# A transformer block on eight cores: where the recurrent scan is cut between the part that runs alone and the part that runs inside the expert layer

## The chip, the cores and the metric

The kernel runs on all 8 cores of one Trainium2 chip. Each core takes one element of the batch (2048 tokens of width 1024) and works alone; nothing is exchanged. The metric is the device time of the slowest core in microseconds (us). The kernel before takes 8822.76 us, the median of three runs (8819.5 to 8960.93).

## The reference, cut to what matters

```
x = layernorm(x + scan_layer(x))          # L0: linear recurrence with tanh, state 128
x = layernorm(x + moe(x))                 # 8 experts, 1024 -> 4096 -> 1024, top 2 of 8
x = layernorm(x + attention(x))           # 16 heads, causal
x = layernorm(x + ffn(x))                 # r * (relu(k)^2 Wv)

def step(state, inp):                     # scan_layer, 2048 steps one after the other
    u_t, sp_t = inp
    state = tanh(state @ A.T + u_t @ B.T) + sp_t
    return state, state @ C.T             # then out = ys @ Wo.T + bo

h = relu(einsum('nd,edh->neh', x_flat, w1) + b1)   # moe: all 8 experts for every token
y = einsum('neh,eho->neo', h, w2) + b2
out = einsum('ne,neo->no', dense_gate, y)
```

Token t of the scan needs token t-1. Everything behind the scan (the output product, the layernorm, the gate, the experts) works on tokens one by one, so tokens whose scan is done can go on while later ones are still being scanned.

## The kernel before, in words

Activations lie with the feature on the partitions: `xA` and `xB` are [128, 8, 2048] fp32, `xS` is the bf16 copy that matmuls read. Tokens are handled in four tiles of 512 (`TS`). Every instruction is written down by the helper `E`, which takes the engine, the operation, the semaphores that it waits for (`w`) and the one it raises (`s`). `realize` then plays one list per engine in the order in which they were written, so the order of the code is the order of every engine's queue. All instructions therefore carry one line number in the profile (L978); groups are told apart by tile names.

- P1: `u`, `sp` and the bias of each step `c` = B u + A sp (shifted by one token) are computed for all 2048 tokens. `sp` and `c` lie in two halves of 1024 columns each (`sp_a`, `sp_b`, `c_a`, `c_b`).
- P2: `scan_step(t)` is one matmul of AT with one column of `tanh_bf` into one of two PSUM columns (TensorE, waits for semaphore `act`), and one tanh of it with bias c into the next column of `tanh_bf` (ScalarE, waits for `spe`). Steps 0 to 1023 run by themselves.
- The loop `for ch in (0, 1)` then takes 1024 tokens (two tiles) at a time through `l0out` (state, C, Wo, residual), `emit_ln` (layernorm), `gate` (router) and `moe`.
- `moe(ch)` walks through 16 halves (8 experts, the hidden width in two halves of 2048). In each half it loads 4 MB of `w1b` and 4 MB of `w2b` (8 DMAs each, counted in bf16, from POOL's queue, each waiting for the one before), and for each tile of the chunk makes 128 matmuls with `w1b` (16 groups of 8, each group evicted through relu by ScalarE and VectorE in turn into `hbuf`) and 128 matmuls with `w2b` (8 groups of 16, evicted by VectorE into `xB`). I call the first 128 the w1 section and the other 128 the w2 section. `w1b` and `w2b` have one buffer each: the next `w1_load` waits for the last w1 matmul of the half (`mm1`), `w2_load` for the last w2 eviction of the half (`ye`). All weights are loaded once for each chunk.
- In chunk 0, `moe` calls `hook()` after each of the 24 groups of a tile. `hook` calls `scan_pump`, which writes as many scan steps as are due: 1024 steps over 768 calls. Steps 1024 to 2047 are so put between the groups of chunk 0's experts. Chunk 1 has no hooks.
- Before chunk 1, columns 1024 to 2047 of `xA` are loaded again by SyncE, and CT2 and WoB2 by POOL, since `moe` had used their place.
- After both chunks: layernorm, attention, feed-forward layer, layernorm, store.

Of the kernel before, what the change touches and what calls it, by code (L numbers as in the profile page):

```python
# [5 lines left out]
F32 = mybir.dt.float32  # L6
# [20 lines left out]
def build(stage=None):  # L27
# [79 lines left out]
    BT = place("BT_s", [128, 128], BF16, W_OFF + 14592)  # L107
    CT = place("CT_s", [128, 128], BF16, B_OFF + 28928)
    CT2 = place("CT2_s", [128, 128], BF16, A_OFF)
    WoB2 = place("WoB2", [128, D], BF16, A_OFF + 256)  # L110
    ident = place("ident_s", [128, 128], F32, W_OFF + 17408)
    zsq0 = place("zsq0", [128, T], BF16, W_OFF)
    zsq1 = place("zsq1", [128, T], BF16, W_OFF + 4096)
# [20 lines left out]
    sp_a = place("sp_a", [128, 1024], F32, B_OFF + 8192)
    sp_b = place("sp_b", [128, 1024], F32, B_OFF + 4096)
    c_a = place("c_a", [128, 1024], F32, B_OFF + 16384)
    c_b = place("c_b", [128, 1024], F32, B_OFF + 12288)
# [122 lines left out]
    for nt in range(NT):  # L260
        b = 2 + nt % 2
        lo = nt * TS
        for dk in range(NCH):
            E("tensor", "matmul", bank(b), WsB[:, dk, :], xS[:, dk, lo:lo + TS],
              start=(dk == 0), stop=(dk == NCH - 1),
              w=((("evs", max(0, V("evs") - 1)),) if dk == 0 else ()),
              s=("mms" if dk == NCH - 1 else None))
        E("vector", "tensor_scalar_add",
          sp_h[nt // 2][:, (nt % 2) * TS:(nt % 2) * TS + TS], bank(b), bsS,
          w=(("mms", V("mms")),), s="evs")  # L270
    E("vector", "tensor_copy", out=sp_bf[:, 0:1024], in_=sp_a,
      w=(("evs", V("evs")),))
    E("vector", "tensor_copy", out=sp_bf[:, 1024:2048], in_=sp_b, s="spb")
    for nt in range(NT):
        b = 4 + nt % 2
        lo = nt * TS
        E("tensor", "matmul", bank(b), BT, u_bf[:, lo:lo + TS], start=True, stop=False,
          w=(("evu", 4), ("spb", V("spb")), ("evc", max(0, V("evc") - 1))))
        if nt == 0:
            E("tensor", "matmul", bank(b)[:, 1:TS], AT, sp_bf[:, 0:TS - 1],  # L280
              start=False, stop=True, s="mmc")
        else:
            E("tensor", "matmul", bank(b), AT, sp_bf[:, lo - 1:lo + TS - 1],
              start=False, stop=True, s="mmc")
        E("vector", "tensor_copy",
          out=c_h[nt // 2][:, (nt % 2) * TS:(nt % 2) * TS + TS], in_=bank(b),
          w=(("mmc", V("mmc")),), s="evc")
    barrier()

# [1 line left out]

    def scan_step(t):
        if t == 0:
            E("scalar", "activation", tanh_bf[:, 0:1], c_a[:, 0:1], AF.Tanh,
              s="act", chain=False)
            return
        cbias = c_h[t // 1024][:, t % 1024:t % 1024 + 1]
        E("tensor", "matmul", ssb[t % 2], AT, tanh_bf[:, t - 1:t],
          start=True, stop=True, w=(("act", t),), s="spe")
        E("scalar", "activation", tanh_bf[:, t:t + 1], ssb[t % 2],  # L300
          AF.Tanh, bias=cbias, w=(("spe", t),), s="act", chain=False)

    mark("P2_scan")
    for t in range(0, 1024):
        scan_step(t)
    scan_cursor = [1024]

    def scan_pump(nsteps):
        t0 = scan_cursor[0]
# [3 lines left out]
        scan_cursor[0] = t1  # L313

    def l0out(ch):
        lo2 = ch * 1024
        E("vector", "tensor_add", state_bf[:, lo2:lo2 + 1024],
          tanh_bf[:, lo2:lo2 + 1024], sp_h[ch],
          w=(("act", 1024 * (ch + 1)),), s="stb")
        stb_t = V("stb")  # L320
        CTu = CT if ch == 0 else CT2
        WoBu = WoB if ch == 0 else WoB2
        for sub in range(2):
            nt = 2 * ch + sub
            b = sub
            lo = nt * TS
            E("tensor", "matmul", bank(b), CTu, state_bf[:, lo:lo + TS],
              start=True, stop=True,
              w=(("stb", stb_t), ("evy", max(0, V("evy") - 1)),
                 ("ldc2", V("ldc2"))), s="mmy")  # L330
            E("scalar", "activation", ys_bf[:, lo:lo + TS], bank(b), AF.Copy,
              w=(("mmy", V("mmy")),), s="evy")
        evy_t = V("evy")
        for o in range(NCH):
            for sub in range(2):
                nt = 2 * ch + sub
                b = 2 + (o * 2 + sub) % 2
                lo = nt * TS
                E("tensor", "matmul", bank(b), WoBu[:, o * 128:(o + 1) * 128],
                  ys_bf[:, lo:lo + TS], start=True, stop=True,  # L340
                  w=(("evy", evy_t), ("evz", max(0, V("evz") - 1))), s="mmz")
                E("vector", "scalar_tensor_tensor", xB[:, o, lo:lo + TS], bank(b),
                  boS[:, o:o + 1], xA[:, o, lo:lo + TS], ALU.add, ALU.add,
                  w=(("mmz", V("mmz")), ("ldx2", V("ldx2"))), s="evz")
        E("vector", "drain", s="l0d")
# [54 lines left out]
        E("vector", "drain", s="lnd")  # L400

    def gate(ch):
        tt0 = 8 * ch
        for tt in range(tt0, tt0 + 8):
            b = 4 + tt % 2
            pt = bank(b)[:, 0:NE]
            lo = tt * 128
            for dk in range(NCH):
                E("tensor", "matmul", pt, xA[:, dk, lo:lo + 128], gwS[:, dk, :],
                  start=(dk == 0), stop=False,  # L410
                  w=((("ggl", max(0, V("ggl") - 1)), ("apl", V("apl")))
                     if dk == 0 else ()))
# [3 lines left out]
        gp3 = gscr[:, 0:64].rearrange("p (t e) -> p t e", t=8)
        gm3 = gscr[:, 512:576].rearrange("p (t e) -> p t e", t=8)
        gx = gscr[:, 256:264].rearrange("p (t o) -> p t o", o=1)
        gv = gscr[:, 768:776].rearrange("p (t o) -> p t o", o=1)
        gsl = glall[:, tt0:tt0 + 8, :]  # L420

        def bc8(ap):
            return ap.to_broadcast([128, 8, NE])

        E("vector", "reduce_max", gx, gsl, AX.X, s="gmx")
        E("vector", "tensor_tensor", gp3, gsl, bc8(gx), ALU.subtract)
# [7 lines left out]
        E("vector", "reduce_max", gv, gm3, AX.X)  # L434
        E("vector", "tensor_tensor", gm3, gp3, bc8(gv), ALU.is_ge)
        E("vector", "tensor_mul", gsl, gp3, gm3, s="gtile")
        for tt in range(tt0, tt0 + 8):
# [6 lines left out]
        E("vector", "tensor_copy", out=xB[:, :, ch * 1024:(ch + 1) * 1024],  # L444
          in_=xA[:, :, ch * 1024:(ch + 1) * 1024], s="zin")

    def w1_load(e, half, w=()):
        for dk in range(NCH):
# [15 lines left out]
    HALVES = [(e, h) for e in range(NE) for h in range(2)]  # L464

    def moe(ch, hook=None):
        nts = (2 * ch, 2 * ch + 1)
        w1_load(HALVES[0][0], HALVES[0][1], w=(("zin", V("zin")),))
        for hi, (e, half) in enumerate(HALVES):
            w1_tgt = V("w1l")  # L470
            ye_at_start = V("ye")
            w2_load(e, half, w=(("ye", ye_at_start),))
            if half == 0:
                cl = ch * 1024
                E("sync", "dma_start", out=row0[:, cl:cl + 1024],
                  in_=g8[e:e + 1, cl:cl + 1024],
                  w=(("gbc", V("gbc")),), s="grw", n=16)
# [591 lines left out]
```

How the kernel before makes its waits and increments, by code:

```python
    def run(eng_obj, lst):  # L969
        eng_key = [k for k, v in ops.items() if v is lst][0]
        for method, args, kw, w, s, n in lst:
            for sn, v in w:
                if v > 0:
                    eng_obj.wait_ge(sems[sn], v)
            if method == "wait_":
                names[eng_key].append(None)
                continue
            ins = getattr(eng_obj, method)(*args, **kw)
            names[eng_key].append(ins.ins.name)
            if s is not None:
                ins.then_inc(sems[s], n)
```

## Time and profile before

| what | us |
|---|---|
| median of 3 runs | 8822.76 |
| lowest, highest | 8819.5, 8960.93 |
| the profiled execution | 8840.08 |
| its span, slowest core (5) | 8838.5 |
| other cores' spans | 8809.8 to 8837.8 |

Busy time of core 5: TensorE matmuls 5711.6 us (65% of the span), weight loads 2411.4, VectorE 2787.7, ScalarE 1527.7, POOL 406.5. The span is read by stage. A row of the windows view gives start and end of the stretch, its length, then the busy time (and number of instructions) of TensorE's matmuls, its weight loads, VectorE, ScalarE and POOL, then the mean granted TensorE clock (1.00 is 2.4 GHz, 0.50 is 1.2 GHz), the mean busy share of the 16 DMA engines, and GB/s. A timeline row gives the start, the duration, the instruction with its count, and in brackets how long the engine had been idle and what released it.

### The profile page before, as it was taken

The numbers are of one execution on the slowest core, as the hardware profiler recorded it, in microseconds if no ns is written. First come the engines' busy times: TensorE is split into PE (matmuls) and PEld (weight loads), VectorE is DVE, ScalarE is ACT, GpSimd is POOL, SyncE is SP. The second block draws the span as 40 slices with busy tenths as digits, with TensorE's granted clock in tenths as the row PEclk, the third lists the DMA queues.
The fourth block names the chain that finished last, engine by engine and source line by source line (L and its number), as shares of the span: only waits on it lengthen the run. The fifth ranks groups of instructions, "written<-read, shape, count | busy, mean of one in ns | idle before, by whom it ended". The sixth has DMA issues, their size and how long they took to land.

```text
span 8838.5 us, 83477 instructions; the slowest of 8 cores (8809.8 to 8838.5 us)
## 1 busy us (share of the span) xinstructions
PE 5711.6 (65%) x24427; PEld 2411.4 (27%) x24427; DVE 2787.7 (32%) x4295; ACT 1527.7 (17%) x3342; POOL 406.5 (5%) x612
## 2 busy tenths in 40 slices
PE   2223588787878785788787878844556455645455
PEld 1112233333333332333333333311112111211122
DVE  0002222222222223222222222245454555455544
ACT  2332111111111111000000000012222211221111
POOL 0000000000000000000000000000000000000000
PEclk6555899999999996899898989965656555655667
DMA  1000333424243430434334343300000000000012
GB/s 44 0 0 0 56 59 51 65 46 65 45 65 48 63 53 26 72 53 62 62 53 71 54 67 57 59 8 8 10 10 5 6 10 10 5 5 5 0 19 48
DMA packets 237365, 319.62 MB, mean 36 GB/s; under 512 B 66198, under 2 KB 197782, under 8 KB 234902
## 3 DMA queue, kind: packets, MB, share of 16 engines
q0 software_dynamic: 226560, 284.33, 21.6%
q1 hardware_dynamic: 10390, 29.94, 1.1%
q8 instruction: 238, 3.90, 0.2%
q14 instruction: 177, 1.45, 0.1%
HBM read 581.62 MB, written 8.39 MB: 67 GB/s over the span
## 4 chain that ended last, share of the span: by engine, by line
PE 42%; DMA 25%; DVE 15%; issue 10%; ACT 7%; DVEq 1%; ACTq 0%; POOLq 0%; SPq 0%; PEldq 0%
PE psA L978 35%; DMA w1b<-w 15%; DMA w2b<-w 8%; PE psB L978 7%; DVE mcols L978 4%; ACT tanh_bf L978 4%; ACT PT L978 2%; DVE xA L978 2%; DVE Qpair L978 1%; DVE qraw L978 1%; DVE mtmp L978 1%; DVE rowT L978 1%; DVE mcol L978 1%; ACT rowT L978 1%; DVE xB L978 1%
## 5 line engine op out<-in xcount | busy, mean ns | idle before, releaser
L978 PE MATMUL psA<-xS,w1b 128*128 128x512 bf16 x8192 | 1880.4, 388 | 566.4 <-DMA w1b<-w 551.7
L978 PE MATMUL psA<-hbuf,w2b 128*128 128x512 bf16 x8192 | 1820.5, 382 | 150.7 <-DVE hbuf L978 73.4
L978 PEld LDWEIGHTS psA<-xS,w1b 128*128 128x128 bf16 x8192 | 775.7, 99 | 1522.7 <-issue 670.2
L978 DVE TENSOR_SCALAR hbuf<-psA,b1c 128x512 bf16<-128x512 f32 x512 | 384.4, 751 | 2260.3 <-PE psA L978 2260.3
L978 PEld LDWEIGHTS psA<-hbuf,w2b 128*128 128x128 bf16 x8192 | 784.8, 98 | 1119.8 <-issue 219.9
L978 PE MATMUL psB<-tanh_bf,AT_s 128*128 128x1 bf16 x2047 | 337.7, 165 | 725.7 <-ACT tanh_bf L978 725.7
L978 ACT ACTIVATE hbuf<-psA,b1c 128x512 bf16<-128x512 f32 x512 | 351.8, 687 | 1631.9 <-PE psA L978 1630.4
L978 ACT ACTIVATE tanh_bf<-psB,c_b 128x1 bf16<-128x1 f32 x1024 | 268.0, 262 | 1307.9 <-PE psB L978 1307.9
L978 ACT ACTIVATE PT<-psA 128x512 bf16<-128x512 f32 (+3 forms) x448 | 308.4, 688 | 1023.0 <-PE psA L978 1011.4
L978 PEld LDWEIGHTS psB<-tanh_bf,AT_s 128*128 128x128 bf16 x2047 | 206.7, 101 | 944.8 <-issue 856.6
L978 DVE SCALAR_TENSOR_TENSOR ytmp<-psA,b2c,g_sb 128x512 f32<-128x512 f32 x256 | 192.3, 751 | 637.6 <-PE psA L978 637.6
L978 DVE SCALAR_TENSOR_TENSOR ytmp<-psA,g_sb 128x512 f32<-128x512 f32 x256 | 177.1, 692 | 648.9 <-PE psA L978 648.9
L978 DVE TENSOR_TENSOR xB<-xB,ytmp 128x512 f32<-128x512 f32 x512 | 354.6, 693 | 55.7 <-DVE ytmp L978 3.2
L978 PE MATMUL psA<-Qh,Kh 65*128 65x512 bf16 (+3 forms) x640 | 258.3, 475 | 164.0 <-ACT PT L978 116.8
L978 ACT ACTIVATE tanh_bf<-psB,c_a 128x1 bf16<-128x1 f32 x1023 | 269.6, 264 | 419.3 <-PE psB L978 419.3
L978 POOL DMA_DIRECT2D w1b<-w x256 | 136.1, 532 | 3878.2 <-PE psA L978 1663.8
L978 PE MATMUL psA<-Kh,Qh 64*128 64x512 bf16 (+1 forms) x320 | 129.0, 524 | 202.3 <-DVE mcols L978 118.5
L978 POOL DMA_DIRECT2D w2b<-w x256 | 190.1, 743 | 1360.6 <-DMA w2b<-w 1152.3
L978 PE MATMUL psB<-PT,Vg 128*65 128x512 bf16 (+3 forms) x640 | 231.4, 471 | 16.9 <-DVE PT L978 7.8
L978 ACT ACTIVATE g_sb<-psB 128x512 f32<-128x512 f32 x64 | 38.2, 597 | 1153.2 <-DVE xB L978 867.0
L978 PE MATMUL psA<-aout,wub 64*128 64x512 bf16 x512 | 219.7, 629 | 22.1 <-DVE aout L978 22.1
L978 PE MATMUL psB<-Kh,Qh 64*128 64x512 bf16 (+1 forms) x320 | 142.7, 567 | 131.6 <-DVE mcols L978 128.4
(157 smaller groups left out, 3685.6 us busy)
## 6 DMA issues: line engine op xcount, KB each, us to landing
w1b<-w POOLq DMA_DIRECT2D x256, 512.0 KB, 5.3
w2b<-w POOLq DMA_DIRECT2D x256, 512.0 KB, 5.4
xA<-xT SPq DMA_DIRECT2D x8, 1024.0 KB, 17.0
out<-ost SPq DMA_DIRECT2D x8, 1024.0 KB, 12.7
xA<-xT SPq DMA_DIRECT2D x8, 512.0 KB, 8.6
Qh<-Qpair SPq DMA_DIRECT2D x16, 256.0 KB, 3.5
Kh<-Qpair SPq DMA_DIRECT2D x16, 256.0 KB, 3.7
wqb<-WqT POOLq DMA_DIRECT2D x16, 128.0 KB, 3.2
```

What stands on the lines that cost most here:

```text
L978: ins = getattr(eng_obj, method)(*args, **kw)
```

## The change

The scan is cut at 512 steps, not at 1024, and the chunks are tiles (0) and (1, 2, 3), not (0, 1) and (2, 3). Steps 0 to 511 run by themselves; the other 1536 are put into chunk 0's experts, which now work on one tile. `hook()` is also called after each of the 8 matmuls of a w1 group, so that there are 16 x 152 = 2432 calls (in each tile of a half 16 x 9 in the w1 section and 8 in the w2 section). `l0out`, `gate` and `moe` take their tiles from `CH_NTS`. `sp` and `c` lie in four pieces of 512 columns, at places that chunk 0 does not write; WoB2 moves to a place that the reload of `xA` (now columns 512 to 2047) leaves free.

```
-    WoB2 = place("WoB2", [128, D], BF16, A_OFF + 256)
+    WoB2 = place("WoB2", [128, D], BF16, A_OFF + 8192)
...
+    CH_NTS = ((0,), (1, 2, 3))
     mark("P2_scan")
-    for t in range(0, 1024):
+    for t in range(0, TS):
         scan_step(t)
-    scan_cursor = [1024]
+    scan_cursor = [TS]
...
     def l0out(ch):
-        lo2 = ch * 1024
-        E("vector", "tensor_add", state_bf[:, lo2:lo2 + 1024],
-          tanh_bf[:, lo2:lo2 + 1024], sp_h[ch],
-          w=(("act", 1024 * (ch + 1)),), s="stb")
-        stb_t = V("stb")
+        nts = CH_NTS[ch]
...
+        for i, nt in enumerate(nts):
+            lo = nt * TS
+            E("vector", "tensor_add", state_bf[:, lo:lo + TS],
+              tanh_bf[:, lo:lo + TS], sp_n[nt],
+              w=((("act", (nts[-1] + 1) * TS),) if i == 0 else ()), s="stb")
...
     def moe(ch, hook=None):
-        nts = (2 * ch, 2 * ch + 1)
+        nts = CH_NTS[ch]
...
                           s=("mm1" if dk == NCH - 1 else None))
+                        if hook is not None:
+                            hook()
...
                 E("sync", "dma_start", out=xA[:, c, TS:T],
                   in_=xT[c * 128:(c + 1) * 128, TS:T], s="ldx2", n=16)
...
-            ngroups = 16 * 2 * 24
+            nhooks = 16 * len(CH_NTS[0]) * (16 * 9 + 8)
             per = [0]
 
             def hook(per=per, ch=ch):
                 if ch == 0:
                     per[0] += 1
-                    tgt = 1024 + (1024 * per[0]) // ngroups
+                    tgt = TS + ((T - TS) * per[0]) // nhooks
                     scan_pump(tgt - scan_cursor[0])
```

TensorE's queue in chunk 0's experts before, from the end of one half into the w1 section of the next (`tanh_bf,AT_s` is a scan step, `w1b` and `w2b` are the experts):

```order
L978 MATMUL psA<-hbuf,w2b 128x512 [waits w2b,ye,hes,hev]
L978 MATMUL psA<-hbuf,w2b 128x512 x15
L978 MATMUL psB<-tanh_bf,AT_s 128x1 [waits act] x2
L978 MATMUL psB<-brow_g,ones_rb 128x512 [waits gcv]
L978 MATMUL psA<-xS,w1b 128x512 [waits w1l,hes]
L978 MATMUL psA<-xS,w1b 128x512 x7
L978 MATMUL psB<-tanh_bf,AT_s 128x1 [waits act]
L978 MATMUL psA<-xS,w1b 128x512 [waits w1l,hev]
```

The same queue now, two groups of a w1 section:

```order
L987 MATMUL psA<-xS,w1b 128x512 [waits w1l,hev]
L987 MATMUL psB<-tanh_bf,AT_s 128x1 [waits act]
L987 MATMUL psA<-xS,w1b 128x512 x2
L987 MATMUL psB<-tanh_bf,AT_s 128x1 [waits act]
L987 MATMUL psA<-xS,w1b 128x512
L987 MATMUL psB<-tanh_bf,AT_s 128x1 [waits act]
L987 MATMUL psA<-xS,w1b 128x512 x2
L987 MATMUL psB<-tanh_bf,AT_s 128x1 [waits act]
L987 MATMUL psA<-xS,w1b 128x512 x2
L987 MATMUL psB<-tanh_bf,AT_s 128x1 [waits act] x2
L987 MATMUL psA<-xS,w1b 128x512 [waits w1l,hes]
```

Where one or two scan steps stood behind every eighth matmul, one now stands behind every first or second. In the w2 section a step still stands only behind a group of 16.

ScalarE's queue there before, and now (`hbuf` is a relu, waiting for its group by `mm1`):

```order
L978 ACTIVATE tanh_bf<-psB,c_b 128x1 [waits spe] x2
L978 ACTIVATE hbuf<-psA,b1c 128x512 [waits mm1,act]
L978 ACTIVATE tanh_bf<-psB,c_b 128x1 [waits spe] x3
L978 ACTIVATE hbuf<-psA,b1c 128x512 [waits mm1,mm2,act]
L978 ACTIVATE tanh_bf<-psB,c_b 128x1 [waits spe] x14
```

```order
L987 ACTIVATE tanh_bf<-psB,c_n_114 128x1 [waits spe] x5
L987 ACTIVATE hbuf<-psA,b1c 128x512 [waits mm1,act]
L987 ACTIVATE tanh_bf<-psB,c_n_114 128x1 [waits spe] x11
L987 ACTIVATE hbuf<-psA,b1c 128x512 [waits mm1,mm2,act]
L987 ACTIVATE tanh_bf<-psB,c_n_114 128x1 [waits spe] x12
```

Between two relus there are now 11 or 12 tanhs where there were 2 or 3; behind the last relu of a tile there are 12 (the rest of the w1 section and the w2 section) where there were 14.

## Rows read from the trace of the kernel before

**Rows 1.** Cores: the slowest, its span and mean granted clock.
```profile
core 5: 8838.5 us, clock 0.768
```

**Rows 2.** Windows by stage: lone scan; chunk 0 before and in experts; chunk 1 likewise.
```profile
83.40:772.00 688.60, 167.09 (x1023) 106.48 (x1023) 0.00 (x0) 269.42 (x1023) 0.00 (x0) 0.50 0.00 0
772.00:954.80 182.80, 72.00 (x227) 41.08 (x228) 59.92 (x100) 14.06 (x16) 4.27 (x8) 0.56 0.14 23
954.80:3366.50 2411.70, 1916.05 (x9246) 854.33 (x9246) 557.86 (x774) 437.42 (x1311) 158.83 (x248) 0.95 0.36 55
3366.50:3569.10 202.60, 73.07 (x229) 41.35 (x230) 61.03 (x102) 14.15 (x16) 5.31 (x10) 0.55 0.20 43
3569.10:5787.00 2217.90, 1848.20 (x8222) 811.90 (x8223) 557.57 (x773) 194.40 (x287) 158.84 (x248) 0.92 0.39 59
```

**Rows 3.** Timeline, TensorE, second tile of one half of chunk 1's experts.
```profile
3771.19 27.80 PE L978 MATMUL psA<-xS,w1b 128*128 128x512 bf16 x128
3800.13 27.79 PE L978 MATMUL psA<-hbuf,w2b 128*128 128x512 bf16 x128 [1.15 <-DVE hbuf L978]
3830.58 0.37 PE L978 MATMUL psB<-brow_g,ones_rb 1*128 1x512 bf16 x1 [2.66 <-DVE brow_g L978]
3845.58 29.07 PE L978 MATMUL psA<-xS,w1b 128*128 128x512 bf16 x128 [14.62 <-DMA w1b<-w]
```

**Rows 4.** Timeline, POOL, the same half: first w1b, first and last w2b issue behind it.
```profile
3799.60 0.54 POOL L978 DMA_DIRECT2D w1b<-w  x1 [49.44 <-PE psA L978]
...
3845.88 0.75 POOL L978 DMA_DIRECT2D w2b<-w  x1 [5.25 <-DMA w1b<-w]
...
3889.20 0.74 POOL L978 DMA_DIRECT2D w2b<-w  x1 [5.29 <-DMA w2b<-w]
```

**Rows 5.** Timeline, chunk 0's experts: a w1b load, and the matmul behind it.
```profile
1364.21 0.54 POOL L978 DMA_DIRECT2D w1b<-w  x1 [62.40 <-PE psA L978]
...
1411.77 3.22 PE L978 MATMUL psA<-xS,w1b 128*128 128x512 bf16 x8 [15.68 <-DMA w1b<-w]
```

**Rows 6.** Timeline, a step of the lone scan, TensorE.
```profile
85.40 0.16 PE L978 MATMUL psB<-tanh_bf,AT_s 128*128 128x1 bf16 x1 [0.51 <-ACT tanh_bf L978]
```

**Rows 7.** Timeline, relu, tanh and the scan step waiting for it, chunk 0's experts.
```profile
1418.70 0.69 ACT L978 ACTIVATE hbuf<-psA,b1c 128x512 bf16<-128x512 f32 x1 [1.56 <-PE psA L978]
1419.28 0.26 ACT L978 ACTIVATE tanh_bf<-psB,c_b 128x1 bf16<-128x1 f32 x1
...
1419.68 0.16 PE L978 MATMUL psB<-tanh_bf,AT_s 128*128 128x1 bf16 x1 [1.19 <-ACT tanh_bf L978]
...
1419.92 0.38 PE L978 MATMUL psA<-xS,w1b 128*128 128x512 bf16 x1
```

**Rows 8.** Timeline, TensorE, a waited-for step ahead of a w2 group; a step between groups.
```profile
1383.93 0.16 PE L978 MATMUL psB<-tanh_bf,AT_s 128*128 128x1 bf16 x1 [0.54 <-ACT tanh_bf L978]
1384.37 3.61 PE L978 MATMUL psA<-hbuf,w2b 128*128 128x512 bf16 x16 [0.28 <-issue]
1387.82 0.17 PE L978 MATMUL psB<-tanh_bf,AT_s 128*128 128x1 bf16 x1
1387.85 3.61 PE L978 MATMUL psA<-hbuf,w2b 128*128 128x512 bf16 x16
```

**Rows 9.** Timeline, chunk 0's first w1 group, at the low clock.
```profile
954.81 3.57 PE L978 MATMUL psA<-xS,w1b 128*128 128x512 bf16 x8 [43.75 <-DMA w1b<-w]
...
958.18 0.21 PE L978 MATMUL psB<-tanh_bf,AT_s 128*128 128x1 bf16 x1
```

**Rows 10.** Windows (columns as in rows 2): an experts tile, l0out, the feed-forward layer.
```profile
1415.00:1478.70 63.70, 55.94 (x276) 25.21 (x275) 15.70 (x22) 12.53 (x38) 5.19 (x7) 1.00 0.45 65
...
3389.00:3401.00 12.00, 7.93 (x15) 1.36 (x13) 10.28 (x14) 0.00 (x0) 0.00 (x0) 0.50 0.00 0
8449.00:8509.00 60.00, 60.00 (x229) 24.84 (x228) 0.00 (x0) 17.23 (x29) 6.11 (x7) 0.81 0.32 31
```

**Rows 11.** Timeline, the first matmul of chunk 1's l0out.
```profile
3386.20 1.01 PE L978 MATMUL psA<-state_bf,CT_s 128*128 128x512 bf16 x2 [19.51 <-DMA WoB<-WoT]
```

More of the change, by code:

```diff
@@ L133, in build @@
     u_bf = place("u_bf", [128, T], BF16, B_OFF)
[L134 to L137, printed above, removed]
+    sp_n = [place("sp_n0", [128, TS], F32, B_OFF + 8192),
+            place("sp_n1", [128, TS], F32, B_OFF + 4096),
+            place("sp_n2", [128, TS], F32, B_OFF + 6144),
+            place("sp_n3", [128, TS], F32, B_OFF + 45056)]
+    c_n = [place("c_n0", [128, TS], F32, B_OFF + 16384),
+           place("c_n1", [128, TS], F32, B_OFF + 12288),
+           place("c_n2", [128, TS], F32, B_OFF + 14336),
+           place("c_n3", [128, TS], F32, B_OFF + 36864)]
     tanh_bf = place("tanh_bf", [128, T], BF16, B_OFF + 20480)
     sp_bf = place("sp_bf", [128, T], BF16, B_OFF + 24576)
-    sp_h = (sp_a, sp_b)
-    c_h = (c_a, c_b)
     w1b = place("w1b", [128, NCH, 2048], BF16, A_OFF)
@@ L267, in build @@
               s=("mms" if dk == NCH - 1 else None))
-        E("vector", "tensor_scalar_add",
-          sp_h[nt // 2][:, (nt % 2) * TS:(nt % 2) * TS + TS], bank(b), bsS,
+        E("vector", "tensor_scalar_add", sp_n[nt], bank(b), bsS,
           w=(("mms", V("mms")),), s="evs")
-    E("vector", "tensor_copy", out=sp_bf[:, 0:1024], in_=sp_a,
-      w=(("evs", V("evs")),))
-    E("vector", "tensor_copy", out=sp_bf[:, 1024:2048], in_=sp_b, s="spb")
+    for nt in range(NT):
+        E("vector", "tensor_copy", out=sp_bf[:, nt * TS:(nt + 1) * TS],
+          in_=sp_n[nt],
+          w=((("evs", V("evs")),) if nt == 0 else ()),
+          s=("spb" if nt == NT - 1 else None))
     for nt in range(NT):
@@ L284, in build @@
               start=False, stop=True, s="mmc")
-        E("vector", "tensor_copy",
-          out=c_h[nt // 2][:, (nt % 2) * TS:(nt % 2) * TS + TS], in_=bank(b),
+        E("vector", "tensor_copy", out=c_n[nt], in_=bank(b),
           w=(("mmc", V("mmc")),), s="evc")
@@ L293, in scan_step @@
         if t == 0:
-            E("scalar", "activation", tanh_bf[:, 0:1], c_a[:, 0:1], AF.Tanh,
+            E("scalar", "activation", tanh_bf[:, 0:1], c_n[0][:, 0:1], AF.Tanh,
               s="act", chain=False)
             return
-        cbias = c_h[t // 1024][:, t % 1024:t % 1024 + 1]
+        cbias = c_n[t // TS][:, t % TS:t % TS + 1]
         E("tensor", "matmul", ssb[t % 2], AT, tanh_bf[:, t - 1:t],
@@ L315, in l0out @@
     def l0out(ch):
-        lo2 = ch * 1024
-        E("vector", "tensor_add", state_bf[:, lo2:lo2 + 1024],
-          tanh_bf[:, lo2:lo2 + 1024], sp_h[ch],
-          w=(("act", 1024 * (ch + 1)),), s="stb")
-        stb_t = V("stb")
+        nts = CH_NTS[ch]
         CTu = CT if ch == 0 else CT2
         WoBu = WoB if ch == 0 else WoB2
-        for sub in range(2):
-            nt = 2 * ch + sub
-            b = sub
+        for i, nt in enumerate(nts):
[3 more added lines that the diff above has]
+              w=((("act", (nts[-1] + 1) * TS),) if i == 0 else ()), s="stb")
+        stb_t = V("stb")
+        for i, nt in enumerate(nts):
+            b = i % 2
             lo = nt * TS
@@ L334, in l0out @@
         for o in range(NCH):
-            for sub in range(2):
-                nt = 2 * ch + sub
-                b = 2 + (o * 2 + sub) % 2
+            for i, nt in enumerate(nts):
+                b = 2 + (o * len(nts) + i) % 2
                 lo = nt * TS
@@ L402, in gate @@
     def gate(ch):
-        tt0 = 8 * ch
-        for tt in range(tt0, tt0 + 8):
+        nts = CH_NTS[ch]
+        tt0 = nts[0] * 4
+        ntt = len(nts) * 4
+        for tt in range(tt0, tt0 + ntt):
             b = 4 + tt % 2
@@ L415, in gate @@
               w=(("gmm", V("gmm")),), s="ggl")
[L416 to L420, printed above, removed]
+        gp3 = gscr[:, 0:8 * ntt].rearrange("p (t e) -> p t e", t=ntt)
+        gm3 = gscr[:, 512:512 + 8 * ntt].rearrange("p (t e) -> p t e", t=ntt)
+        gx = gscr[:, 256:256 + ntt].rearrange("p (t o) -> p t o", o=1)
+        gv = gscr[:, 768:768 + ntt].rearrange("p (t o) -> p t o", o=1)
+        gsl = glall[:, tt0:tt0 + ntt, :]
         def bc8(ap):
-            return ap.to_broadcast([128, 8, NE])
+            return ap.to_broadcast([128, ntt, NE])
         E("vector", "reduce_max", gx, gsl, AX.X, s="gmx")
@@ L436, in gate @@
         E("vector", "tensor_mul", gsl, gp3, gm3, s="gtile")
-        for tt in range(tt0, tt0 + 8):
+        for tt in range(tt0, tt0 + ntt):
             lo = tt * 128
@@ L443, in gate @@
               w=(("gtr", V("gtr")),), s="gev")
-        E("vector", "tensor_copy", out=xB[:, :, ch * 1024:(ch + 1) * 1024],
-          in_=xA[:, :, ch * 1024:(ch + 1) * 1024], s="zin")
+        E("vector", "tensor_copy",
+          out=xB[:, :, nts[0] * TS:(nts[-1] + 1) * TS],
+          in_=xA[:, :, nts[0] * TS:(nts[-1] + 1) * TS], s="zin")
     def w1_load(e, half, w=()):
@@ L466, in moe @@
     def moe(ch, hook=None):
-        nts = (2 * ch, 2 * ch + 1)
+        nts = CH_NTS[ch]
         w1_load(HALVES[0][0], HALVES[0][1], w=(("zin", V("zin")),))
@@ L473, in moe @@
             if half == 0:
-                cl = ch * 1024
-                E("sync", "dma_start", out=row0[:, cl:cl + 1024],
-                  in_=g8[e:e + 1, cl:cl + 1024],
+                cl = nts[0] * TS
+                cw = len(nts) * TS
+                E("sync", "dma_start", out=row0[:, cl:cl + cw],
+                  in_=g8[e:e + 1, cl:cl + cw],
                   w=(("gbc", V("gbc")),), s="grw", n=16)
-                E("vector", "tensor_copy", out=brow_g[:, cl:cl + 1024],
-                  in_=row0[:, cl:cl + 1024],
+                E("vector", "tensor_copy", out=brow_g[:, cl:cl + cw],
+                  in_=row0[:, cl:cl + cw],
                   w=(("grw", V("grw")), ("gbc", V("gbc"))), s="gcv")
@@ L536, in build @@
     if stage < 4:
-        scan_pump(1024)
+        scan_pump(T - TS)
     for ch in (0, 1):
@@ L540, in build @@
             for c in range(NCH):
-                E("sync", "dma_start", out=xA[:, c, 1024:2048],
-                  in_=xT[c * 128:(c + 1) * 128, 1024:2048], s="ldx2", n=16)
+                E("sync", "dma_start", out=xA[:, c, TS:T],
+                  in_=xT[c * 128:(c + 1) * 128, TS:T], s="ldx2", n=16)
             E("gpsimd", "dma_start", out=CT2, in_=CT_d, s="ldc2", n=16)
@@ L547, in build @@
         mark(f"ln1_c{ch}")
-        emit_ln(xB, xA, xS, "l1", nts=(2 * ch, 2 * ch + 1),
+        emit_ln(xB, xA, xS, "l1", nts=CH_NTS[ch],
                 after=(("l0d", V("l0d")),))
@@ L564, in build @@
             if ch == 0:
-                scan_pump(2048 - scan_cursor[0])
+                scan_pump(T - scan_cursor[0])
             barrier()
```

## The prediction, on record before the changed kernel ran

> **What bounds the kernel now.** I read the cores first: the slowest, core 5, has 8838.5 us at a mean clock of 0.768 [rows 1], and the others come within 29 us of it, so its trace stands for all. Then the windows by stage [rows 2]. The change touches five of them: the lone scan (688.6 us), what lies ahead of chunk 0's experts (182.8), chunk 0's experts (2411.7), ahead of chunk 1's (202.6), chunk 1's experts (2217.9). The reader is to see that the lone scan moves nothing but two small instructions in turn, at the low clock and with no DMA, while the experts have TensorE busy for 1916 and 1848 us out of 2412 and 2218. What the experts' idle time is made of is in the timeline of one half. In chunk 1 the second tile's w1 section ends at 3799, only then is the next w1b load issued (3799.60), and its eight DMAs, one behind another, are done at 3845.58, where the next half starts [rows 3, 4]. The w2 section, 27.8 us, lies beside that load of 46.0 us; the rest of the load is waiting. In chunk 0 the same load took 47.56 us [rows 5]. I use 46.8.
>
> So each half costs its w1 sections, its w2 sections but the last, and a w1b load that hides the last w2 section. The wait for w1b is paid once a half and chunk, whatever number of tiles the chunk has. This is why moving a tile from one chunk to the other is no gain by itself, and the question is what the scan steps cost in their new places.
>
> **The lone scan.** 1023 steps take 688.6 us, 0.673 us each [rows 2]; one step shows it, 0.51 us of waiting for the tanh and 0.16 of matmul [rows 6]. 512 fewer: **-344.6 us**.
>
> **Chunk 1's experts get a third tile.** It costs 16 times a tile without waits for DMA. From rows 3: w1 section 27.80, wait for the last relu 1.15, w2 section 27.79, gate row 0.37: 57.1 us, times 16 = **+914 us**. Nothing hides it, since the w1b load starts behind the last w1 section as before, and the second w1 section already ran at full speed.
>
> **Chunk 0's experts lose a tile and get more steps.** Call M the time of the w1 section with its scan steps. POOL issues the w1b load 1.0 us behind it and the next half starts 46.8 later; the w2 section (27.8 us and 6 steps) lies beneath. The last half has no load behind it but its w2 section, 32.4 us with the wait ahead of it. So the stage is 15 x (M + 47.8) + M + 32.4 = 749 + 16 M. The w2b load needs from 3845.88 to about 5.9 us behind 3889.20, 49 us [rows 4], and is hidden as long as M is more than that. It is: by the order 90 steps stand in a w1 section, 42 of them behind two matmuls, 44 behind one, 4 behind none.
>
> Below, M is bounded by the chain of steps. Matmul, tanh and both semaphores take 0.67 us at an otherwise idle TensorE [rows 6]. At 2.4 GHz a w1 matmul takes 0.217 us (27.80 / 128, rows 3), two of them 0.43 and so fit into the time in which TensorE waits for the tanh anyway: 90 x 0.67 = 60.3. Relus share ScalarE with the tanhs. A tanh behind a relu starts 0.58 us after the relu's start, and in the case shown the next step waited 1.19 us where it waits 0.51 in the lone scan, 0.68 late [rows 6, 7]. Eight relus a section cost between 0 and 5.4 us. I take 2, as most steps reach ScalarE at another moment: M = 62.
>
> Above, it is the clock. At 1.2 GHz a matmul takes (958.18 - 954.81) / 8 = 0.42 us [rows 9], two with the step's own 0.03 to 0.05 take 0.89 and are longer than the chain. 42 x 0.89 + 48 x 0.67 = 69.5. What does the restart behind a waited-for step cost? 0.24 us where the next matmul has two semaphores to wait for (1419.68 to 1419.92), 0.44 where it has four (1384.37), 0.03 where TensorE had not waited [rows 7, 8]. That is 0.1 us a semaphore and next to nothing without one. Only the 16 group heads have semaphores: at most 16 x 0.2 = 3.2 us. M = 73.
>
> Which clock will it be? Every half begins at the low one, because TensorE sits idle for the rest of the load. With full groups of eight it was 1.00 afterwards, with a step between them; in l0out, where a matmul and an eviction alternate, it stayed at 0.50, and so it did in the lone scan [rows 2, 10]. The new section lies between: matmuls fill 28 of 62 us at the high clock and 54 of 73 at the low one. No row shows this mixture. I take the middle, **M = 67**, and keep 61 and 80 as ends.
>
> The Trainium skill has a rule that speaks against the change (TensorE: Matmul & The Clock Gate, "A second HAM failure mode: psum-queue depth-cycling"): short idle moments between groups of matmuls can make the clock swing between its two levels, and throughput falls although the matmuls at the high level look the same. It would put M between my two values; always low is the first rival below. The rows agree with it for l0out and do not decide it here.
>
> 749 + 16 x 67 = 1821 against 2411.7: **-591 us**.
>
> **Stages ahead of the experts.** Work per tile is the same in sum. Chunk 1's first matmul waits 19.5 us for WoB2 [rows 11], a load beside which `xA` is reloaded; that reload grows from 4 to 6 MB and may end some us later. 0 to +12, I take **+4**. The smaller copies in P1 are of equal total size: 0.
>
> **Sum.** -344.6 + 914 - 591 + 4 = -18 us. The profiled execution (8840.1) becomes 8822; it stood 17.3 over the median, and from the median 8822.8 I get **8805 us**. Each us of M is worth 16. About 2% (176 us) is what a measurement of this kernel can tell from no change.
>
> **Rivals.**
>
> *The section runs cold and each restart costs (the other side).* If TensorE stays at 1.2 GHz through the w1 sections, and a restart behind a waited-for step costs 0.24 us in every place and not only at group heads, a pair of matmuls takes 0.24 + 0.84 = 1.08: 42 x 1.08 + 48 x 0.67 + 3 = 80.5. That gives 8805 + 13.5 x 16 = 9021, slower by 2.2%. It decides from M = 79 on (8823 + 176 = 8999). For it: the low clock at the start of each half, the order in which every step is waited for. Against it: the restart row with two semaphores is the only one near, and the high clock came back behind every load so far. Cold but with cheap restarts (M = 73) gives 8901, still within 2%.
>
> *The chain is the only limit.* The high clock returns at once and the relus fall into gaps: M = 61.5, 8805 - 5.5 x 16 = 8717. For it: the rows with groups of eight. Against it: no rest for relus. More than this cannot be had, as 90 steps at 0.67 are 60.3 us.
>
> *Chunk 1 meets a lower clock.* In the feed-forward layer, the longest run of matmuls without a wait, the granted clock was 0.81 [rows 10], and 229 matmuls in 60 us are 0.262 each. With three tiles chunk 1's dense stretches grow from 72 to 130 us. If its 3 x 256 matmuls a half ran so, 16 x 768 x 0.045 = +553 us, 9358. Against it: a dense tile of the experts had 1.00 for 63.7 us, as long as that window [rows 10], and chunk 1's stage has 0.92 as its mean with the waits in it [rows 2]. The skill's page on TensorE names in Part 1 a limit by current at 13/16 of the clock with three or more cores of a die busy; the 0.81 row agrees.
>
> *It does not do what it says.* If steps were left over behind chunk 0 they would run at 0.67 us each. By the count 16 x 96 = 1536 none are.
>
> **Chances.** Forecast with M from 62 to 76 (8725 to 8949): 0.70. Cold and costly restarts (9021 and around): 0.11. Chain alone (8717 and a little below): 0.12. Lower clock in chunk 1: 0.03. Something unseen: 0.04, half of it faster. Over 2% faster than before needs M below 57, under the floor of the chain: 0.04. Slower by over 2%: 0.11 + 0.03 + 0.01, as 0.15. The rest, 0.81, is within 2%. The range reaches from M = 61 (8709) to M = 76 (8949).
>
> **What would show it.** The lone scan ends near 428 us. Halves of chunk 0 come every 115 us (110 if the chain alone counts, 121 if cold, 128 with costly restarts), those of chunk 1 every 196 to 198. The wait for w1b in chunk 0 stays near 17 us a half. Windows of a w1 section in chunk 0 show a mean clock between 0.5 and 1.0. The prediction is wrong if a scan step between matmuls takes more than 0.88 us on the mean, if TensorE waits for w2b in chunk 0, or if the clock in chunk 1 falls to 0.81.

## The result, and the profile after

The changed kernel takes **0.9911** of the time of before (95% interval 0.9871 to 0.9951). From 8822.8 us that is 8744 us, 79 us less (43 to 114 less). I had forecast 18 us less, that is, no change one could tell from noise; the change is small, but its interval leaves 1.0 out. In a second set of runs the ratio was 0.9944 (0.9905 to 0.9984).

I read core 5 of the profiled execution (span 8787.2 us). That was one of the longer executions, which the ratio leaves out: its granted clock was 0.81 for parts of the time and 0.754 on the mean of core 5, where the executions that the ratio compares have 0.77 to 0.79; so chunk 1's experts are read once more below from experiment e2, where the code of that chunk is the same and the cores ran alike.

The windows by stage, with the columns of [rows 2]: lone scan, ahead of chunk 0's experts, chunk 0's experts, ahead of chunk 1's, chunk 1's experts.

```profile
83.40:428.00 344.60, 83.15 (x510) 53.04 (x510) 0.00 (x0) 135.60 (x512) 0.00 (x0) 0.50 0.00 0
428.00:552.60 124.60, 38.34 (x115) 20.80 (x115) 31.50 (x60) 9.26 (x15) 4.26 (x8) 0.53 0.20 34
552.60:2309.40 1756.80, 1342.54 (x5646) 448.68 (x5647) 278.64 (x389) 489.01 (x1679) 158.84 (x248) 0.81 0.49 75
2309.40:2574.50 265.10, 108.35 (x344) 61.70 (x343) 90.04 (x144) 19.04 (x17) 5.31 (x10) 0.56 0.18 41
2574.50:5770.90 3196.40, 2867.30 (x12335) 1241.86 (x12335) 836.60 (x1157) 292.00 (x431) 159.48 (x248) 0.91 0.27 41
```

And chunk 1's experts in e2's trace, core 5:

```profile
2653.60:5771.60 3118.00, 2736.79 (x12335) 1210.60 (x12335) 836.53 (x1157) 292.77 (x431) 160.09 (x248) 0.95 0.27 42
```

| stage | before [rows 2] | after | difference | forecast |
|---|---|---|---|---|
| lone scan | 688.6 | 344.6 | -344.0 | -344.6 |
| ahead of the experts, both chunks | 385.4 | 389.7 | +4.3 | +4 |
| chunk 0's experts | 2411.7 | 1756.8 | -654.9 | -591 |
| chunk 1's experts (e2's trace) | 2217.9 | 3118.0 | +900.1 | +914 |
| sum | | | -94.5 | -18 |

The sum lies inside the measured interval, 15 us from the 79 that the ratio gives; which stage those are in I do not know. It rests on e2's row: with the changed kernel's own row for chunk 1 (+978.5) it would be -16. The stages behind chunk 1 have the same code in both kernels and still took 3051.5 us in the trace of before and 3016.3 in this one, so two single traces compare no better than that. The lone scan and the stages ahead of the experts came out to within 1 us. Most of the difference from the forecast stands in one row: chunk 0's experts are 64 us shorter than I said.

Inside a half the reader is to look at the scan steps. Timeline of the changed kernel, core 5, TensorE and ScalarE, in a w1 section at a granted clock of 0.81:

```profile
672.03 0.16 PE L987 MATMUL psB<-tanh_bf,AT_s 128*128 128x1 bf16 x1 [0.22 <-ACT tanh_bf L987]
672.05 0.42 PE L987 MATMUL psA<-xS,w1b 128*128 128x512 bf16 x1
672.29 0.26 ACT L987 ACTIVATE tanh_bf<-psB,c_n 128x1 bf16<-128x1 f32 x1 [0.41 <-PE psB L987]
672.70 0.16 PE L987 MATMUL psB<-tanh_bf,AT_s 128*128 128x1 bf16 x1 [0.22 <-ACT tanh_bf L987]
...
672.93 0.42 PE L987 MATMUL psA<-xS,w1b 128*128 128x512 bf16 x1
...
673.37 0.16 PE L987 MATMUL psB<-tanh_bf,AT_s 128*128 128x1 bf16 x1
673.39 0.69 PE L987 MATMUL psA<-xS,w1b 128*128 128x512 bf16 x2
```

The steps come at 672.03, 672.70 and 673.37: 0.67 us apart, exactly the pace of the lone scan [rows 6]. One matmul or two fit in between. Behind a waited-for step the next matmul starts 0.02 us later where it has no semaphore (672.03 to 672.05), and 0.23 later at a group head (672.70 to 672.93), as [rows 7] had it. The clock of a w1 section on core 2, where it was never 0.81 in this stage, first over the whole section and then without its first 4 us; the third row is the same section on core 5:

```profile
662.80:725.00 62.20, 45.39 (x211) 13.79 (x215) 5.25 (x7) 27.83 (x96) 5.86 (x8) 0.97 0.48 68
667.10:725.00 57.90, 41.28 (x199) 12.51 (x203) 5.25 (x7) 26.41 (x91) 5.20 (x7) 1.00 0.46 66
664.50:727.40 62.90, 50.93 (x216) 13.98 (x217) 5.26 (x7) 27.85 (x97) 5.94 (x8) 0.79 0.48 68
```

On core 2 it was 2.4 GHz behind the first 4 us. On core 5 the section had 0.79 on the mean and took 0.7 us more. There, in the second half, the section ran from 664.46 to the start of its last matmul at 727.4, and then POOL could begin with w1b, which ends the half:

```profile
664.46 1.01 PE L987 MATMUL psA<-xS,w1b 128*128 128x512 bf16 x2 [13.16 <-DMA w1b<-w]
...
775.28 1.01 PE L987 MATMUL psA<-xS,w1b 128*128 128x512 bf16 x2 [9.59 <-DMA w1b<-w]
```

```profile
728.46 0.54 POOL L987 DMA_DIRECT2D w1b<-w  x1 [19.59 <-PE psA L987]
...
769.84 0.53 POOL L987 DMA_DIRECT2D w1b<-w  x1 [5.35 <-DMA w1b<-w]
775.58 0.75 POOL L987 DMA_DIRECT2D w2b<-w  x1 [5.21 <-DMA w1b<-w]
```

M, the w1 section, is 62.9 us here (62.5 to 64.1 in the 16 halves; I had taken 67), the load 46.8 as assumed, the half 110.8 on the mean. Two of the signs that I had named came out as said: TensorE waits for no w2b in chunk 0, and it waits 17 us a half for w1b on core 2. On core 5 it waits only 12, since the w2 section, at a clock of 0.81, is longer beneath the same load; the half is not.

### The profile page after: what moved, and what is told of

The parts are those of the page before. It is cut to its first block, busy times and chain, and to the rows that moved or that the text cites. A ratio compares the mean times of both kernels' runs of the same rounds, so it can differ in the third digit from the quotient of the medians.

```text
span 8949.7 us, 83494 instructions; the slowest of 8 cores (8787.2 to 8949.7 us)
## 1 busy us (share of the span) xinstructions
PE 6122.9 (68%) x24427; PEld 2406.7 (27%) x24427; DVE 2786.9 (31%) x4299; ACT 1542.3 (17%) x3342; POOL 404.9 (5%) x612
## 4 chain that ended last, share of the span: by engine, by line
PE 48%; DMA 20%; DVE 15%; issue 9%; ACT 7%; DVEq 1%; ACTq 0%; POOLq 0%; SPq 0%; PEldq 0%
PE psA L987 40%; DMA w1b<-w 15%; PE psB L987 8%; DVE mcols L987 4%; ACT tanh_bf L987 4%; DMA w2b<-w 3%; ACT PT L987 2%; DVE xA L987 1%; DVE Qpair L987 1%; DVE qraw L987 1%; DVE mtmp L987 1%; DVE rowT L987 1%; DVE mcol L987 1%; ACT rowT L987 1%; DVE xB L987 1%
## 5 line engine op out<-in xcount | busy, mean ns | idle before, releaser
L987 PE MATMUL psA<-xS,w1b 128*128 128x512 bf16 x8192 | 2186.7, 408 | 566.7 <-DMA w1b<-w 548.1
L987 PE MATMUL psA<-hbuf,w2b 128*128 128x512 bf16 x8192 | 1926.9, 401 | 94.1 <-DVE hbuf L987 70.5
L987 PEld LDWEIGHTS psA<-hbuf,w2b 128*128 128x128 bf16 x8192 | 823.9, 102 | 1173.4 <-issue 563.5
L987 ACT ACTIVATE tanh_bf<-psB,c_n 128x1 bf16<-128x1 f32 x2047 | 538.8, 263 | 1432.1 <-PE psB L987 1432.1
L987 ACT ACTIVATE g_sb<-psB 128x512 f32<-128x512 f32 x64 | 38.2, 597 | 1734.9 <-DVE xB L987 1425.8
L987 PE MATMUL psA<-xrk,wfb 128*128 128x512 bf16 x512 | 134.8, 435 | 134.2 <-DVE xrk L987 134.1
```

The source lines that it names most:

```text
L987: ins = getattr(eng_obj, method)(*args, **kw)
```

## The experiments

Two theories. **A, the chain:** the section lasts as long as its scan steps, 0.67 us each, plus some us for the relus, and the clock does not enter as long as two matmuls fit between two steps. **B, the clock and the restarts:** what lies between the steps sets the section, and the clock swings.

### e1: hooks in both sections

```
                           s=("mm2" if hk == 15 else None))
+                        if hook is not None:
+                            hook()
-            nhooks = 16 * len(CH_NTS[0]) * (16 * 9 + 8)
+            nhooks = 16 * len(CH_NTS[0]) * (16 * 9 + 8 * 17)
```

> Edit: hook() also after each of the 128 w2 matmuls, so 96 steps are spread over 280 calls: 49 in the w1 section, 47 in the w2 section. Theory A (the w1 section lasts as long as its chain of steps, 0.67 us each plus about 2.5 for the relus, at any clock of 2 GHz or more; behind it comes the w1b load): w1 section 49 x 0.67 + 2.5 = 35 us instead of 62.9. The w1b load can then not start 1 us behind the section, since POOL is still loading w2b until 49 us into the half: a half takes 49 + 46.8 = 96 us instead of 110.7. Total 14.7 x 15 + 27 = about 245 us less than the changed kernel, near 8480. Theory B (TensorE's clock or its restarts set the section, the chain does not): more steps in the w2 section cost there what they save here, and a half stays within 5 us of 110. Theory C (the load of w1b is not hidden beside a denser w2 section and gets slower): halves of 100 us or more with w1b DMAs over 6.5 us apart.

Measured: 8456.0 us, **0.9618** of before (0.9574 to 0.9662). w1 section 38.2 us, half 94.8 (core 5). Theory A held for the time (8480 expected) and for the half; the section was 3 us longer than 35 (2 of them went with the relus in e6; the rest is open). What now sets the half is in POOL's rows of e1, which leave no gap between w1b and w2b:

```profile
782.00 0.74 POOL L989 DMA_DIRECT2D w2b<-w  x1 [6.36 <-DMA w2b<-w]
788.08 0.54 POOL L989 DMA_DIRECT2D w1b<-w  x1 [5.35 <-DMA w2b<-w]
795.16 0.54 POOL L989 DMA_DIRECT2D w1b<-w  x1 [6.54 <-issue]
...
829.97 0.53 POOL L989 DMA_DIRECT2D w1b<-w  x1 [5.32 <-DMA w1b<-w]
835.69 0.75 POOL L989 DMA_DIRECT2D w2b<-w  x1 [5.20 <-DMA w1b<-w]
```

The first w1b issue waits for the last w2b and no longer for TensorE. Sixteen DMAs 5.9 us apart are the 95 us. So the changed kernel put 90 of its 96 steps where they were on the path to the next load, and 6 where 47 cost nothing.

### e2: all steps in the w1 section

```
                       xB[:, o, lo:lo + TS], ytmp, s="ye")
-                    if hook is not None:
-                        hook()
-            nhooks = 16 * len(CH_NTS[0]) * (16 * 9 + 8)
+            nhooks = 16 * len(CH_NTS[0]) * (16 * 9)
```

> Edit: no hook() in the w2 section, 96 steps over 144 calls, all in the w1 section (90 before the edit). Theory A: six more steps are six times 0.67: w1 section 66.9 us instead of 62.9, half 114.7, total +60 to +64 us against the changed kernel (about 8785 to 8790). Theory B: the matmuls between the steps are the same 128, so the section stays at 63 to 64 us and the total within 15 us.

Measured: the two lowest runs 8781.6 and 8811.1 us, no ratio. The sections give the answer: 67.2 to 68.2 us as the median of a core, half 115.5 to 116.1 as the mean of a core. Six more steps made 4.3 to 5.3 us of section; A says 4.0. Theory B's "63 to 64" is out. But there is a remainder of up to 1.3 us, and the clock is in it. One section of e2, core 5, and a stretch inside it:

```profile
784.30:852.30 68.00, 49.74 (x221) 15.02 (x222) 5.25 (x7) 29.39 (x101) 5.95 (x8) 0.89 0.43 62
798.80:805.60 6.80, 5.85 (x21) 1.80 (x22) 0.75 (x1) 2.13 (x8) 0.75 (x1) 0.50 0.68 100
```

Over the whole section the granted clock was 0.89 where the changed kernel had 0.97 on core 2: it fell to 0.50 inside the section. Why it does so with 96 steps and hardly with 90, no run shows. At the low clock two matmuls no longer fit. In the timeline of e2, two matmuls behind the step at 800.45 hold back the next one until 801.28, 0.83 us later:

```profile
800.45 0.16 PE L985 MATMUL psB<-tanh_bf,AT_s 128*128 128x1 bf16 x1
800.47 1.02 PE L985 MATMUL psA<-xS,w1b 128*128 128x512 bf16 x2
...
801.28 0.21 PE L985 MATMUL psB<-tanh_bf,AT_s 128*128 128x1 bf16 x1
```

### e3: the split alone

```
                           s=("mm1" if dk == NCH - 1 else None))
-                        if hook is not None:
-                            hook()
-            nhooks = 16 * len(CH_NTS[0]) * (16 * 9 + 8)
+            nhooks = 16 * len(CH_NTS[0]) * 24
```

> Edit: the cut at 512 and the chunks of the changed kernel, but hook() only after each group as before the change (24 calls a tile and half), so steps come in bunches of 4. Theory A with the steps serial inside a bunch: w1 section 27.8 + 16 x (3 x 0.67 + 0.3 + 0.23) + 3 = 71 us, and the w2 section 27.8 + 8 x 2.6 = 48.6 us, now as long as the w1b load: half 119 to 122 us, total 130 to 180 us more than the changed kernel (8855 to 8905), so the tile split alone is no gain over before. Theory B: bunches leave TensorE idle for 2 us at a time, the clock may fall to 1.2 GHz, section 85 us or more, half over 133, total over 9080.

Measured: 9308.5 us, **1.0536** of before (1.0479 to 1.0592). Section 84.7 us, half 142.8 (core 5). Here theory B won: A's 71 us, which assumed the high clock, is 14 short. The windows of one section, of two stretches inside it, and of the w2 section behind it:

```profile
692.40:777.30 84.90, 55.21 (x188) 21.36 (x188) 5.25 (x7) 21.33 (x70) 5.94 (x8) 0.66 0.34 50
692.40:702.10 9.70, 5.79 (x30) 2.69 (x30) 0.75 (x1) 3.44 (x11) 1.50 (x2) 1.00 0.45 65
702.10:715.70 13.60, 9.69 (x30) 3.45 (x27) 0.75 (x1) 2.71 (x9) 1.48 (x2) 0.50 0.63 94
780.10:833.40 53.30, 40.02 (x156) 16.52 (x157) 9.69 (x14) 7.46 (x28) 3.71 (x7) 0.84 0.46 78
```

and a bunch in the timeline (e3, TensorE):

```profile
721.39 0.21 PE L985 MATMUL psB<-tanh_bf,AT_s 128*128 128x1 bf16 x1
...
722.14 0.16 PE L985 MATMUL psB<-tanh_bf,AT_s 128*128 128x1 bf16 x1 [0.54 <-ACT tanh_bf L985]
...
722.81 0.16 PE L985 MATMUL psB<-tanh_bf,AT_s 128*128 128x1 bf16 x1 [0.51 <-ACT tanh_bf L985]
...
723.48 0.16 PE L985 MATMUL psB<-tanh_bf,AT_s 128*128 128x1 bf16 x1 [0.51 <-ACT tanh_bf L985]
723.71 3.57 PE L985 MATMUL psA<-xS,w1b 128*128 128x512 bf16 x8
```

Two us with nothing but scan steps, then eight matmuls at the low clock (3.57 us). The mean granted clock was 0.66 in the section, and it swung between 1.00 and 0.50. An estimate from these rows: a bunch takes 2.3 us and eight matmuls 1.7 at the high or 3.4 at the low clock, so that a mean of 0.66 stands for some ten of 16 groups at the low one, 81 us; with A's 3 us for relus that is 84. A half has the same 256 matmuls and 96 steps as in the changed kernel; only their order differs, and with it the split (64 and 32 steps in the two sections, not 90 and 6).

The rule of the Trainium skill that I had set against the change (TensorE: Matmul & The Clock Gate, "A second HAM failure mode: psum-queue depth-cycling") says that short idle moments between groups of matmuls make the clock swing between its two levels. The trace of e3 agrees, and that of e2 in small part (0.89). The row of l0out that I had counted for it does not show this: 0.50 throughout is low, but no swing.

### e4: the hooks alone

```
-    CH_NTS = ((0,), (1, 2, 3))
+    CH_NTS = ((0, 1), (2, 3))
-    for t in range(0, TS):
+    for t in range(0, 2 * TS):
...
-                    tgt = TS + ((T - TS) * per[0]) // nhooks
+                    tgt = 2 * TS + ((T - 2 * TS) * per[0]) // nhooks
```

(The reload of `xA` and the places of `sp`, `c` and WoB2 go back to those of before with it.)

> Edit: hook() after each w1 matmul as in the changed kernel, but the cut at 1024 and the chunks (0, 1) and (2, 3) of before. 64 steps a half over 304 calls, one behind every fourth or fifth matmul, 0.9 us apart and so longer than the chain. Theory A: each step costs TensorE 0.03 us and no wait; w1 sections 28.7 and 29.5 us where before had 34.4 and 36.6; half 141.5 us instead of 151.75, total 150 us less than before the change (about 8670), more than the whole change brought. Theory B: TensorE restarts at each step, 0.2 us each, half 153, total as before.

Measured: **0.9793** of before (0.9764 to 0.9821), lowest run 8613.5 us. w1 sections of 29.1 to 31.4 us where before had 34.3 to 37.5, half 139.8 where before had 151.8 (core 5). As theory A said; the half came out 1.7 us shorter still, and the total about 182 us below before where 150 were expected. That it is faster is clear of noise; whether by 2%, the interval leaves open. In the timeline (e4, TensorE) a step costs 0.03 us and waits for nothing:

```profile
1027.52 0.17 PE L987 MATMUL psB<-tanh_bf,AT_s 128*128 128x1 bf16 x1
1027.55 0.81 PE L987 MATMUL psA<-xS,w1b 128*128 128x512 bf16 x3
```

So of the two parts of the change, the finer hooks by themselves bring 2.1%, the split by itself loses 5.4%, and together they bring 0.9%.

### e5 and e6: the relus

```
+                        hval = V(hsem)
+                        if ch == 0:
+                            hsem, hval = "hev", max(0, V("hev") - 1)
...
-                          w=((("w1l", w1_tgt), (hsem, V(hsem)))
+                          w=((("w1l", w1_tgt), (hsem, hval))
...
-                    if hk % 2 == 0:
+                    if hk % 2 == 0 and ch == 1:
```

> Edit: in chunk 0 all 16 relus of a section are made by VectorE, none by ScalarE, so that nothing stands between two tanhs. Theory A: the 2.6 us over 90 x 0.67 = 60.3 are the relus: section 60.4 us instead of 62.9, half 108.2, total 40 us less than the changed kernel. Rival: the 2.6 us are TensorE's start at the low clock and the group heads' semaphores: section stays at 62.5 or more, total within 10 us of it.

Measured: 0.9894 of before (0.9802 to 0.9987), lowest run 8672.9 us against 8718.4 of the changed kernel in the same set. Section 60.5 to 60.7 us as the median of each core whose records are complete, half 108.3 to 109.0. So 2.3 of the 2.6 us above the chain were the relus. What is left is 90 x 0.67 to within 0.3.

e6 is the same edit on e1.

> Edit: hooks in both sections (as in e1) and all relus of chunk 0 on VectorE. Theory A: in e1 a half is POOL's 16 DMAs, 95.6 us, and no longer the section, so a shorter section (38.1 us to 35) changes nothing: half 95.6, total within 15 us of e1 (8440 to 8470). Rival (the section still counts in e1): half 93, total 40 us less.

Measured: 0.9587 (0.9559 to 0.9615), lowest run 8426.6. Section 36.1 us, 2 us less than in e1, half 94.4 where e1 had 94.8: no use, as expected, since POOL's DMAs set the half. The spans of core 5 are 8421.7 and 8448.8, 27 us apart. By stage only 9 of them are in chunk 0's experts (1485.3 against 1494.7 us); 12 are in chunk 1's and 5 behind them, whose code the edit does not touch. So no more than 9 us can be the edit's.

### e7: no steps in the experts

```
-            moe(ch, hook=hook)
+            moe(ch)
```

> Edit: no hook in chunk 0; the 1536 steps run by themselves behind chunk 0's experts. Theory A: a half of chunk 0 without any step is POOL's 16 DMAs too, 95.6 us, the same as with 96 steps spread over both sections (e1), so e1 has its steps for nothing. Total e1 + 1536 x 0.673 = 8450 + 1034 = 9484, within 30 us. Rival: steps cost something in e1: half under 93 us.

Measured: one run, 9513.8 us, 30 over the 9484 expected; core 5 spans 9449.9. Halves of chunk 0 of 94.5 to 95.0 us on the mean of a core. With 96 steps a half (e1) it was 94.8 to 95.5. The steps are free in e1 to within 1 us a half. In e7 the first w1b matmul of a half waits 29 us for its DMA:

```profile
642.86 29.68 PE L987 MATMUL psA<-xS,w1b 128*128 128x512 bf16 x128 [29.07 <-DMA w1b<-w]
```

### r1: the changed kernel again

> No edit: the changed kernel once more, for rows of an execution in which all cores of a die run alike and for its ratio beside the others of this set. Theory A: w1 sections of chunk 0 at 62.5 to 63.5 us, half 110 to 111, granted clock 1.00 in the section behind its first few us, time 8720 to 8745. Theory B (the clock swings between its two levels in the section): sections that differ by more than 3 us from one half to the next.

Measured: 0.9944 (0.9905 to 0.9984), lowest run 8718.4. Sections 62.4 to 64.1 us on all cores whose records are complete, halves 110.4 to 110.9. They do not differ by 3 us, so B's picture of a swinging clock is out for this kernel. Of the changed kernel's first trace that holds too but for the first section of two cores (66.0 and 65.8 us). The clock of 1.00 behind the first few us was there in nearly every section on cores 6 and 7 alone; the others had 0.81 in half or more of their sections, at the same length. In chunk 1 it was 0.81 as well, so this trace gives no better row for that chunk.

### e8: loads that do not wait for one another

```
-              w=(w if dk == 0 else ()), s="w1l", n=16)
+              w=(w if dk == 0 else ()), s="w1l", n=16,
+              chain=(dk == 0))
...
-                  s=("w2a" if oc == 0 else "w2b"), n=16)
+                  s=("w2a" if oc == 0 else "w2b"), n=16,
+                  chain=(oc == 0 and hg == 0))
```

> Edit on e6: the eight DMAs of a w1b load, and of a w2b load, no longer wait for one another (only the first waits for what it waited for). Theory A (in e1, e6 and e7 a half of chunk 0 is POOL's row of 16 DMAs, each waiting for the one before, 5.9 us each; the 16 DMA engines themselves were less than half busy): with the eight in flight together a load takes 20 to 30 us, below a section; a half of chunk 0 is 36 + 1.5 + 33 + 1 = about 72 us instead of 94.4, a half of chunk 1 about 174 instead of 195: total about 8425 - 22 x 16 - 21 x 16 = 7735 us. Rival (the loads are bound by memory or by the DMA engines): a load still takes 45 us or more, halves and total within 2% of e6.

Measured: the runs lie apart (7707.1 to 8217.4) and give no ratio; the two lowest are 7707.1 and 7775.6 us, the lowest of before in that set 8801.6, a quotient of 0.876 for the lowest. The halves are 70.5 us in chunk 0 and 173.2 in chunk 1 (core 5), where 72 and 174 were expected. POOL's rows, e8, core 5, the first one with the matmul that waits for it, ahead of chunk 0's experts:

```profile
502.21 4.27 POOL L994 DMA_DIRECT2D w1b<-w  x8 [458.81 <-DVEq L994]
530.11 1.44 PE L994 MATMUL psA<-xS,w1b 128*128 128x512 bf16 x3 [25.32 <-DMA w1b<-w]
...
602.67 5.99 POOL L994 DMA_DIRECT2D w2b<-w  x8 [30.75 <-DVE xB L994]
637.08 4.26 POOL L994 DMA_DIRECT2D w1b<-w  x8 [28.42 <-PE psA L994]
672.21 5.96 POOL L994 DMA_DIRECT2D w2b<-w  x8 [30.87 <-DVE xB L994]
```

and the windows of one half of chunk 0 and of chunk 1:

```profile
600.00:671.00 71.00, 65.23 (x357) 23.71 (x354) 23.93 (x34) 26.33 (x99) 10.21 (x16) 1.00 0.80 119
3000.00:3173.00 173.00, 169.56 (x782) 75.85 (x781) 52.33 (x73) 19.57 (x29) 10.22 (x16) 1.00 0.31 49
```

Eight DMAs are issued within 4 to 6 us, and a load of w1b takes 28 us from its first issue (502.21 to 530.11) where the same load took 47 in e6. TensorE is busy for 65 of 71 and 170 of 173 us at a clock of 1.00, and the DMA share in chunk 0 rises to 0.80. It was 0.57 in e6, not less than half as I had written. The wait for w1b that every half and chunk had paid was POOL waiting for each DMA before it issued the next.

## Why the prediction was wrong, point by point

- **The lone scan**, 512 steps at 0.673: -344.6 said, -344.0 measured. Right.
- **The stages ahead of the experts**, +4 said, +4.3 measured. Right.
- **The third tile in chunk 1**, 57.1 us each, +914 said; +900 measured in e2's trace, the halves 56.2 us longer (196.0 against 139.8). Right in kind, 14 us too dear.
- **The model of a half in chunk 0**, M + 47.8: right. With M = 62.9 it gives 110.7, and 110.8 was measured.
- **M = 67 was the step that failed.** I had 62 for the chain at the high clock and 73 for the low one, and took the middle because no row showed the mixture. It measured 62.9. Sixteen times the 4.1 us are 66 us, which is the missing sum: with 62.9 the forecast would have been -84 us, 8739. What ran is my own lower bound, the chain with its relus: 60.6 us without them (e5), 62.9 with them, where I had 60.3 and 2 more. The clock entered the sum where it had no place: it was at 2.4 GHz behind the first 4 us (core 2), and where 0.81 was granted instead (core 5) a pair of matmuls still ended before the next step was due. In mechanism that is the rival that I gave a chance of 0.12, the chain as the only limit, though the time is 27 us over its 8717. Both 62.9 and 8744 also lie in the band that I gave 0.70 (M from 62 to 76), at its fast end; that is the width of the band and not a right M.
- **The bounds of M** were both real, but not for the same order of instructions. The chain as a floor stands to 0.3 us (e5: 60.6). The low clock is what e3 ran into (0.66, 84.7 us) with the steps in bunches, and e2 began to run into (0.89) with 96 steps instead of 90. The changed kernel (0.97) lies close to e2 and yet keeps the chain's pace; what decides between them stays open.
- **Costly restarts**: the rule read from [rows 7, 8], 0.1 us a semaphore and next to nothing without one, held (0.02 and 0.23). The rival built on restarts had no ground.
- **A lower clock in chunk 1** was my third sign of a wrong prediction, and the changed kernel's own trace has it in part: 3196.4 us at a mean of 0.91, 78 more than e2's 3118 at 0.95, and far from the 553 of the rival. Dense work does not bring it by itself: in e8 chunk 1 had the three tiles, TensorE busy for 170 of 173 us, and the clock at 1.00 for those 173 us, on all eight cores. What brings the 0.81 stays open.
- **The framing** was too narrow. I bounded M from both sides and did not ask why it was on the path. It was there because POOL's load waits for it, and the same steps in the w2 section lie beneath that load (e1: 0.962).

## What to carry to other kernels

A chain of small dependent steps woven into dense work cost next to nothing here where the work between two steps was longer than the chain's round trip (e4: 0.03 us a step), and the full round trip where it was shorter (0.67), so first put the steps beneath whatever the engine waits for anyway. Spread them evenly: 64 steps in bunches made a section of 85 us where 90 spread ones made 63, because the clock fell as well. Before moving work around a wait, look at what the wait is made of: here it was a queue of DMAs that each waited for the last, and letting them overlap took the lowest run down by 720 us against e6 (8426.6 to 7707.1), nine times what the change brought.

## What the runs showed of the hardware that was not expected

- The granted clock was sensitive to small differences in the mixture. Over a whole w1 section, its slow first us with it: 90 steps among 128 matmuls 0.97 (core 2), 96 steps among the same 0.89, 64 steps in 16 bunches 0.66.
- Between 1.00 and 0.81 the section did not change (62.8 us on core 5, 62.5 on core 7 of the same execution), since two matmuls of 0.26 us [rows 10] still fit into 0.67.
- With eight DMAs in flight the DMA engines were 80% busy and moved 119 GB/s, where an unbroken row of single ones had 0.57 and 89 in e6.
